# Decoder layer on one core: VectorE instead of ScalarE copies the turned context sum in the attention loop

## The reference

```python
query = jnp.einsum('bqi,ih->bqh', image_features, Wq) + bq        # 16 x 56 x 128
key = jnp.einsum('bkt,th->bkh', text_features, Wk) + bk           # 16 x 1500 rows of 96 features
value = jnp.einsum('bkt,th->bkh', text_features, Wv) + bv
scores = jnp.einsum('bqh,bkh->bqk', query, key) * scale
weights = jax.nn.softmax(scores, axis=-1)
attended = jnp.einsum('bqk,bkh->bqh', weights, value)
```

## Time and profile before

| | |
|---|---|
| median of 3 runs | 235.29 us |
| the three runs | 233.55, 235.29, 236.84 us |
| the profiled execution | 235.1 us |
| its span in the trace | 233.3 us |
| PE, DVE, ACT, POOL busy | 203.6, 181.8, 139.4, 33.5 us |
| mean granted TensorE clock | 0.973 of full speed |

### The profile page before, as it was taken

The page is one execution under the profiler, slowest core; times in us unless marked ns, Lnnn a source line. Parts: engine busy times, 40 slices in busy tenths (PEclk is TensorE's granted clock), DMA queues, the critical chain, the costliest instruction groups (busy, mean ns, idle before and its releaser), DMA issues. The chain is left out here.

```text
span 233.3 us, 4964 instructions
## 1 busy us (share of the span) xinstructions
PE 203.6 (87%) x1802; PEld 138.6 (59%) x1802; DVE 181.8 (78%) x430; ACT 139.4 (60%) x268; POOL 33.5 (14%) x48
## 2 busy tenths in 40 slices
PE   7899999767999877889878986999999999999920
PEld 6354555522536464566566745777787777777920
DVE  3859999987896774566776599588888888987894
ACT  2469798224534232442342645598988988898653
POOL 9472000000300001101212170000000000001520
PEclk9999999989999999999999997999999999999995
DMA  5999999006630988693611100031121301000002
GB/s 150 317 234 275 273 239 318 22 0 154 158 85 7 312 262 220 233 238 134 215 37 48 45 3 0 0 93 46 49 48 42 90 9 36 0 0 3 0 0 80
DMA packets 7808, 26.11 MB, mean 112 GB/s; under 512 B 928, under 2 KB 1312, under 8 KB 7792
## 3 DMA queue, kind: packets, MB, share of 16 engines
q1 hardware_dynamic: 7792, 25.89, 39.4%
HBM read 25.43 MB, written 0.46 MB: 111 GB/s over the span
## 5 line engine op out<-in xcount | busy, mean ns | idle before, releaser
L839 ACT ACTIVATE terms<-bank,b_now 128x448 f16<-128x448 f32 x64 | 40.6, 634 | 12.7 <-PE bank L551 12.7
L572 PE MATMUL bank<-w2h,terms 128*128 128x128 f16 x256 | 44.4, 219 | 0.0
L572 PE MATMUL bank<-w2l,terms 128*128 128x128 f16 x256 | 44.3, 219 | 0.0
L572 PE MATMUL bank<-w2h,sums 128*128 128x128 f16 x256 | 44.3, 219 | 0.0
L1226 DVE TENSOR_TENSOR sums<-pc,terms 128x448 f16<-128x448 f32 x60 | 37.0, 620 | 9.4 <-ACT pc L847 9.4
L847 ACT ACTIVATE pc<-bank,b_now 128x448 f32<-128x448 f32 x64 | 40.6, 635 | 0.0
L551 PE MATMUL bank<-turned_late,w1h 128*128 128x448 f16 x128 | 34.7, 353 | 0.0
L572 PEld LDWEIGHTS bank<-w2h,terms 128*128 128x128 f16 x256 | 25.0, 98 | 4.8 <-issue 2.9
L572 PEld LDWEIGHTS bank<-w2l,terms 128*128 128x128 f16 x256 | 25.0, 98 | 1.9
L439 PE MATMUL bank<-ctxT_slot,w_conv 97*64 97x500 f32 (+1 forms) x96 | 23.5, 629 | 1.9 <-ACT pc L763 1.4
L572 PEld LDWEIGHTS bank<-w2h,sums 128*128 128x128 f16 x256 | 25.0, 98 | 0.0
(11 more groups left out here) (173 smaller groups left out, 343.9 us busy)
## 6 DMA issues: line engine op xcount, KB each, us to landing
ctx_slot<-ctx SPq DMA_DIRECT2D x16, 576.0 KB, 5.3
ctxT_slot<-ctx_T SPq DMA_DIRECT2D x16, 562.5 KB, 8.2
w_raw<-w SPq DMA_DIRECT2D x16, 256.0 KB, 2.6
convw_sb<-conv_w SPq DMA_DIRECT2D x3, 256.0 KB, 6.0
small_sb<-small SPq DMA_DIRECT2D x1, 609.0 KB, 9.6
xpad<-x_T SPq DMA_DIRECT2D x2, 236.0 KB, 5.5
xtok<-x_tok SPq DMA_DIRECT2D x1, 448.0 KB, 11.2
out<-x SPq DMA_DIRECT2D x2, 224.0 KB, 2.3
```

The lines of the kernel that those rows point to most:

```text
L572: mm = pe.matmul(bank[:, to, j * D:(j + 1) * D], h_[:, s, f, i, :], w_[:, s, f, :], start=(f == 0 and k == 0), stop=(f == FC - 1 and k == 2))
L839: nc.scalar.activation(hh[:, s, f, c * PPH:(c + 1) * PPH, 0:PT], bank[:, n % 4, 0:HW] .rearrange("p (j t) -> p j t", j=PPH), ACT.Relu, sca ...
```

## The change

In turns 1 to 7 the copy of the transposed context sum leaves ACT's list, where it stood behind ACT's third of the transposed weights, and joins DVE's, between its own two thirds. The last one, behind the loop, stays on ACT under a new name. PE and POOL have the same lists as before, and so has SP.

```diff
-            def turned_sum(i):
+            def last_turned_sum(i):
                 act.wait_ge(a_ut, i + 1)
                 nc.scalar.copy(uT_sb[:].rearrange("d (j l) -> d j l", j=2),
...
                 if i:
-                    turned_sum(i - 1)
                     if i == 1:
                         mix_inv_std(2)
                     attended_inv_std(i - 1)
...
-            turned_sum(PAIRS - 1)
+            last_turned_sum(PAIRS - 1)
...
+            def turned_sum(i):
+                dve.wait_ge(a_ut, i + 1)
+                V.tensor_copy(uT_sb[:].rearrange("d (j l) -> d j l", j=2),
+                              bank[0:DC + 1, TURN_BANK, 256:256 + 2 * GAP]
+                              .rearrange("d (j l) -> d j l", j=2)[:, :, 0:L]).then_inc(a_utsb, 1)
+
             def turned_copy(i):
                 for n in (0, 1):
+                    if n and i:
+                        turned_sum(i - 1)
                     dve.wait_ge(a_t, 3 * i + n + 1)
```

## The result

| | before | with the change |
|---|---|---|
| median | 234.93 us (6 runs) | 228.82 us (6 runs) |
| range | 233.55 to 236.84 | 226.91 to 230.74 |
| ratio | | 0.9725, 95% interval 0.9657 to 0.9792 |
| profiled execution / its span | 235.1 / 233.3 us | 228.34 / 226.5 us |

The account below looks back on a forecast made before the run. PE bounds the kernel, its largest attention wait being for ScalarE's `uT_sb` copy; 0.62 + 0.96 + 3.32 = 4.9 us off 235.1 gives 230.2, plus 0.2 for the median: 230.4, range 228.4 to 232.2.

Parts of the forecast that it names:

- the first rival: Start of the experts: the clock's fall, up to 1.65 us of PE work, stays away, giving 228.7; chance 0.17.
- What bounds the kernel: Attention loop: PE is busy 203.6 of 233.3 us; its largest wait there is for `uT_sb`, 6.4 us.
- Turns 4 to 7: Attention: VectorE's copy starts 0.57 after its first, takes 0.27; PE loads `values` 0.83 us earlier each turn, 3.32 together.
- Turn 3: Attention: `uT_sb` is there before PE is free, so PE's own order ends last; 0.96 us gained.
- Turn 2: Attention: scores then wait for ScalarE's read of the last queries (L754), starting 0.62 us earlier.
- Turn 1: Attention: PE's load waits little and the chain behind it is untouched by the copy; gain and cost 0.
- Sum: At the start of the experts: 0.62 + 0.96 + 3.32 = 4.9 us, carrying to the end.
- What the copy holds up on VectorE: VectorE's second `ph` copy comes 0.27 later, 0.18 us of cover left before `x2T_copy`; cost 0, at most 0.8 us.
- the dearer hand-over on VectorE: Turns 4 to 7: late release or long read costs 0.38 us a turn, time 232.0; chance 0.20.
- Falls inside the attention: Attention: clock falls cost up to 1.65 us each; with four the time is 237.0; chance 0.03.
- A measured gain beyond 2%: Whole kernel: faster by over 2%, 4.7 us or 230.6; chance 0.36 + 0.17 = 0.53.

Follow-up runs that it names:

- first comparison: The changed kernel against the kernel before, six executions each: 228.82 us against 234.93, ratio 0.9725.
- The run set back to the old distance: Changed kernel with 15 warming products (matmuls, results unused) at the head of TensorE's turn 7, delaying it about 5.02 us: 235.68 us, ratio to before 1.0034.
- the kernel before with 1.24 us added: Kernel before with 5 warming products (matmuls, results unused) at the head of TensorE's turn 7: 234.36 us, ratio to before 0.996.
- the second: The changed kernel run once more against the kernel before on the same chip: 229.64 us against 236.2, ratio 0.9768.
- filled: Six more warming products (results unused) ahead of TensorE's routing-weights wait: kernel before 232.13 us, changed kernel 227.71, changed kernel with last queries' read moved ahead 226.29.
- the changed kernel set back by 3.89 us: Changed kernel with 12 warming products (matmuls, results unused) at the head of TensorE's turn 7: 235.67 us.

## Why the prediction was right, and where it was not

The time (230.4 forecast, 228.82 measured) lay in the range of 228.4 to 232.2, and the way and the mechanism in the attention were those forecast. The number itself is off by 1.6 us, and what it hit is the first rival's 228.7, which had a chance of 0.17: the range held it because that rival had set its lower end. Of the 1.6, 0.15 are a larger gain in the attention, about 1.0 the clock's falls, and 0.4 that before's median came out at 234.93 and not at 235.29.

- *What bounds the kernel*: right. PE's wait for `uT_sb`, 6.4 us in the earlier trace rows, is gone, and the time went with it.
- *Turns 4 to 7*, 0.83 each, 3.32: measured 0.85 each, since the scores behind turns 3 and 4 now start 6.77 us apart (95.83 to 102.60) instead of 7.62 (97.61 to 105.23); the run with these turns alone gave 3.39. The start of the copy (0.57 forecast, 0.58) and its length (0.27, 0.26) held. PE's load, for which I had some 0.15 us of standing left, follows 0.13 behind the loads before it, and the profile names no wait. VectorE's seven copies have a median of 0.264 us against ScalarE's 0.257, so of the difference of 0.016 that I had charged from the 128 x 112 copy less than half was there. The rule of the Trainium skill on which engine sits closer to which memory ("VectorE: DVE Perf Modes", Specifications) agrees in sign; what it is worth here is 0.007 us a turn.
- *Turn 3*, 0.96: measured 1.02 (7.06 us between the two starts of scores instead of 8.08).
- *Turn 2*, 0.62 with the query read as the new wait: measured 0.63 (3.98 from L422 to the scores instead of 4.61), with the wait where it was named.
- *Turn 1*, nothing: right; the run with turns 1 to 3 gained 1.64, which is what turns 2 and 3 give (0.63 + 1.02).
- *Sum* 4.9: measured 5.05. Shown by the distance in the trace; the executions without a fall agree with 5.1, on the estimate of 232.0 for before.
- *What the copy holds up on VectorE*, nothing: right. The maximum still waited for PE, 0.66 us at the head of turn 5 and 0.22 at the head of turn 6, and ahead of `x2T_copy` 0.17 us of cover was left where I had 0.18.
- *The clock at the start of the experts*: here a step failed. I gave the fall that stays away a chance of 0.17, priced it at 1.65 us, and held that "the shift is as likely to bring a fall as to remove one, and the median stays". The price was right (1.63). The median didn't stay: it fell by about a microsecond more than the distance did (first comparison). That the Trainium skill's window runs freely ("TensorE: Matmul & The Clock Gate", Part 1) agrees with executions of one kernel lying on several steps; it does not follow that two places where PE stands fall independently. In 68 executions of the kernel before at least one of them always did. The reading that fits the runs is that the distance between the places counts, which is fixed in the program, and that the change altered it. The run set back to the old distance bears it out (0 of 12 without a fall, and before's steps), and so does the kernel before with 1.24 us added (3 of 12); by what working the distance acts, no run here shows.
- *The other rivals*: the dearer hand-over on VectorE didn't happen (0.26 us a copy). Falls inside the attention didn't happen in the profiled execution, whose clock was full from 56 to 126 us. A measured gain beyond 2% I held at 0.53, as a close call with 4.9 against 4.7; it was 2.75% in this comparison and 2.3%, with an interval across 2%, in the second.

What stays open: which distances are good. The kernels with a gain of 0 and of 3.4 us had no execution without a fall (0 of 92 with the one set back), and all others had some, 14 of 52 in the seven that weren't filled; four to twelve executions each are too few to rank them. And why the changed kernel set back by 3.89 us had four such long executions (clock 0.960 to 0.968) was not looked into.

## What to carry to other kernels

When an engine waits for a small result, look at what stands ahead of the instruction that makes it, before looking at the instruction: here the data lay ready 0.93 us while ScalarE waited for something later, and moving the copy ahead on ScalarE alone brought 4.89 of the 5.05 us. Compare such changes by a distance between two instructions in the trace, from a point ahead of the change to one behind it; the medians of two runs with gains of 3.39 and 1.64 us came out in the wrong order. And where TensorE stands at several places and its clock falls behind them, as here behind 2.82 us, fill such a wait (one line, worth the 1.63 us of one fall in the trace) before comparing anything, since moving one place against the other went with a change in how often the clock fell.

## What the runs showed of the hardware

- Granted clock and time are tied closely: a fit over all executions of the study gives 0.43 us more for each microsecond at half clock, with 0.44 us of scatter around it.
- One program's executions lie on a few steps, each with a clock of its own to the third digit, and which steps occurred went with how far apart the standstills lie: 0 of 68 without a fall before, 3 of 12 with 1.24 us of useless work added between them, 2 of 6 with the changed kernel set back by 3.89 us and 0 of 12 with it set back by 5.02.
- A wait of 2.82 us ahead of the routing product was followed by a fall in six kept traces and by none in five others (filled kernels apart); a fall there cost 1.63 us between the routing product and the next hidden layer (5.57 against 3.94 us).
- VectorE and ScalarE read the 97 x 112 tile from the accumulator memory in nearly the same time, 0.264 and 0.257 us.
